# Cross-attention and routed FFN megakernel on one core: answers added one stage earlier, norm 1's moments and the gate in the first batch, one expert product ahead of a wait, the last count one stage later

## The reference, cut to what matters

```python
x = x + xattn(layernorm(x), ctx)        # 16 heads of 64: q = x@Wq, k = ctx@Wk, v = ctx@Wv, softmax, @Wo + bo
x = x + ffn(layernorm(x))               # shared FFN 256->1024->256, plus one of two experts, chosen per token
x = x + attn(layernorm(x), ctx, ctx)    # one head, row mask
x = x + int8_linear(layernorm(x))       # one scale from the largest |value| over all tokens
```

## Time and profile before

| | us |
|---|---|
| runs | 930.33, 926.52, 930.88; median 930.33 |
| the profiled execution's own time | 930.73 |
| its span, first to last instruction | 929.0 |
| TensorE matmul busy | 891.2 (96%) |
| VectorE, ScalarE, GpSimd busy | 595.6, 538.3, 262.0 |
| mean granted TensorE clock | 0.990 |
| chain that ended last | TensorE 90%, VectorE 6%, ScalarE 2%, issue 1%, DMA 1% |

### The profile page before, as it was taken

The page is one execution under the profiler, slowest core; times in us unless marked ns, Lnnn a source line. Parts: engine busy times, 40 slices in busy tenths (PEclk is TensorE's granted clock), DMA queues, the critical chain, the costliest instruction groups (busy, mean ns, idle before and its releaser), DMA issues.

```text
span 929.0 us, 19551 instructions
## 1 busy us (share of the span) xinstructions
PE 891.2 (96%) x6634; PEld 783.2 (84%) x6634; DVE 595.6 (64%) x1603; ACT 538.3 (58%) x1285; POOL 262.0 (28%) x354
## 2 busy tenths in 40 slices
PE   5999999999999999999999999999989999999994
PEld 4788888898888998898889889887878999997763
DVE  6578765666666667666666666665654666437767
ACT  4665556555655656656556555665652455356875
POOL 1343234334433333432434334333000000033200
PEclk9999999999999999999999999999999999999997
DMA  9302000000000000000000000000352043345522
GB/s 277 113 27 109 1 19 22 7 17 5 17 5 21 17 5 17 5 21 17 5 17 5 21 17 5 1 7 6 108 172 85 1 131 126 111 144 163 167 71 80
DMA packets 29500, 50.22 MB, mean 54 GB/s; under 512 B 2960, under 2 KB 24112, under 8 KB 27680
## 3 DMA queue, kind: packets, MB, share of 16 engines
q1 hardware_dynamic: 27920, 45.97, 16.0%
q0 software_dynamic: 1536, 3.67, 1.3%
HBM read 41.37 MB, written 8.26 MB: 53 GB/s over the span
## 4 chain that ended last, share of the span: by engine, by line
PE 90%; DVE 6%; ACT 2%; issue 1%; DMA 1%; another core or an unknown queue 0%; POOL 0%; DVEq 0%
PE bank L1863 27%; PE bank L1892 10%; PE bank L2020 9%; PE bank L2108 9%; PE bank L1911 8%; PE bank L1877 8%; PE bank L1932 5%; PE bank L1836 4%; PE bank L2196 2%; PE bank L2214 2%; PE bank L1845 1%; DVE neg_max L1299 1%; PE bank L1809 1%; PE bank L2072 1%; DVE k_parts L1290 1%
## 5 line engine op out<-in xcount | busy, mean ns | idle before, releaser
L774 POOL TENSOR_TENSOR probs<-probs,row_rcp 112x375 f32<-112x375 f32 x256 | 209.1, 840 | 391.9 <-DVE row_rcp L1305 390.2
L900 ACT ACTIVATE probs<-bank,neg_max 112x375 f32<-112x375 f32 x256 | 144.5, 570 | 56.3 <-DVE neg_max L1299 56.2
L1892 PE MATMUL bank<-ident,probs 112*125 112x112 f32 x768 | 129.2, 278 | 4.0 <-DVE probs_t L1310 4.0
L1892 PEld LDWEIGHTS bank<-ident,probs 112*125 112x125 f32 x768 | 113.3, 187 | 21.3 <-issue 6.2
L1299 DVE TENSOR_REDUCE neg_max<-bank 112x1 f32<-112x375 f32 x256 | 123.3, 540 | 11.1 <-PE bank L1877 10.9
L1310 DVE COPY probs_t<-bank 125x336 f32<-125x336 f32 x128 | 64.8, 507 | 61.1 <-PE bank L1892 57.1
L872 ACT ACTIVATE k_parts<-bank 128x376 fp32r<-128x376 f32 x128 | 62.1, 486 | 66.9 <-PE bank L1863 66.8
L1863 PE MATMUL bank<-ctx_hi,down_hi 128*128 128x376 f32 x256 | 96.7, 378 | 0.5 <-DVE q_parts L1286 0.3
L875 ACT ACTIVATE v<-bank 125x512 f32<-125x512 f32 x96 | 57.5, 599 | 65.1 <-PE bank L1863 65.1
L1290 DVE TENSOR_TENSOR k_parts<-bank,k_parts 128x376 fp32r<-128x376 f32 x128 | 69.9, 547 | 29.6 <-ACT k_parts L872 28.4
L1911 PE MATMUL bank<-probs_t,v 125*64 125x112 f32 x1536 | 87.7, 263 | 0.0
(11 more groups left out here) (237 smaller groups left out, 1984.6 us busy)
## 6 DMA issues: line engine op xcount, KB each, us to landing
ctx_raw<-in_ctx_t SPq DMA_DIRECT2D x16, 375.0 KB, 3.4
stage<-in_ffn_up SPq DMA_DIRECT2D x5, 1024.0 KB, 5.3
stage<-in_ffn_down SPq DMA_DIRECT2D x5, 1024.0 KB, 6.8
ring_late<-in_ctx_t SPq DMA_DIRECT2D x10, 375.0 KB, 6.2
ring_late<-in_ctx_n SPq DMA_DIRECT2D x10, 375.0 KB
routed<-xn SPq DMA_DIRECT2D x1, 2240.0 KB, 9.4
rows_in<-routed SPq DMA_DIRECT2D x5, 448.0 KB, 6.5
answers<-y_rows SPq DMA_DIRECT2D x10, 224.0 KB, 2.8
```

Source lines behind the costliest of these rows:

```text
L774: eng.tensor_tensor(probs[s][:, :], probs[s][:, :], row_rcp[:, s:s + 1].broadcast_to([S, C]), ALU.mult).then_inc(probs_ready, 1)
L900: eng.activation(probs[r][:, :], SCORE_BANKS[i][0:S, 0:C], ACT.Exp, bias=neg_max[:, r:r + 1], accum_out=row_sum[:, r:r + 1]).then_inc(exp_ ...
L1892: t = eng.transpose(turn_bank(i, project)[0:CJ, j * S:(j + 1) * S], probs[QUAD * v + i][:, j * CJ:(j + 1) * CJ], ident[0:S, 0:S])
```

## The change

It has seven edits, in the order of the diff:

- `NORM1_AT`: statistics of step 5 and the aggregations of step 6 move from visit (1, 0, 0) to visit (0, 1, 1), behind step 4.
- ScalarE, s = 1, m = 6: `rows_out(2)` goes ahead of the weight half that is rounded in the same stage.
- VectorE, visit (0, 0, 1): `probs_out(.., 0)` goes ahead of the second pair of row maxima.
- VectorE: the gate's two operations move from visit (1, 0, 0) to visit (0, 1, 1).
- VectorE, `finish_attention`: the places move from n = 4 to n = 5, behind the `idle_*` operations; TensorE's count moves from m = 4 to m = 5.
- VectorE: `y_update` is run at `turn_y_stage(s)` and no longer a stage later (s = 1: m = 4; s = 2: m = 6; s = 8: m = 4), and stands ahead of `piece_lo`, `choose_experts`, `expert_biases` and the norm 3 operations; `rows_rest(2)` goes ahead of `piece_lo`.
- TensorE, visit (15, 1, 1): `up(0, 0)` goes ahead of the wait for ScalarE's copy; `project_out` stays behind it.

```diff
--- before.py
+++ after.py
@@ -557,9 +557,8 @@
         HALF_AT = {1: ("wq", 0), 2: ("wq", 1), 3: ("wo", 0), 4: ("wo", 1), 4 * B - 6: ("up", 0), 4 * B - 5: ("up", 1)}
 
 
-        NORM1_AT = {(0, 0, 1, 0): (0,), (0, 0, 1, 1): (1,), (0, 1, 0, 0): (2,), (0, 1, 1, 0): (3,), (0, 1, 1, 1): (4,),
-                    (1, 0, 0, 0): (5,), (1, 0, 0, 1): (6,), (1, 0, 1, 0): (7,), (1, 0, 1, 1): (8,), (1, 1, 0, 0): (9,),
-                    (1, 1, 1, 0): (10,), (1, 1, 1, 1): (11,)}
+        NORM1_AT = {(0, 0, 1, 0): (0,), (0, 0, 1, 1): (1,), (0, 1, 0, 0): (2,), (0, 1, 1, 0): (3,), (0, 1, 1, 1): (4, 5, 6),
+                    (1, 0, 1, 0): (7,), (1, 0, 1, 1): (8,), (1, 1, 0, 0): (9,), (1, 1, 1, 0): (10,), (1, 1, 1, 1): (11,)}
 
         def half_of(b, c, v, ago):
 
@@ -1053,6 +1052,8 @@
             for s in range(NS):
                 for m in range(MT):
                     relu(s, m)
+                    if m == turn_rows_stage(s) + 1 and s + 1 == FIRST_SLOT:
+                        rows_out(s + 1)
                     if (s, m) in SPLIT_AT:
                         i, h = SPLIT_AT[s, m]
                         if i >= CHOSEN_PIECE:
@@ -1065,7 +1066,7 @@
                         y_out(s - 1)
                     if m == turn_y_stage(s) + 1 and is_slot(s - 1):
                         y_rows_out(s - 1)
-                    if m == turn_rows_stage(s) + 1 and is_slot(s + 1):
+                    if m == turn_rows_stage(s) + 1 and is_slot(s + 1) and s + 1 > FIRST_SLOT:
                         rows_out(s + 1)
                     if s == NS - 1 and m in (5, 6):
                         normalise_group(0, m - 5)
@@ -1353,8 +1354,12 @@
                         rest = rest_for(b, c)
                         if v == 0 and rest is not None:
                             pair_rest(rest, rest % 2 if isinstance(rest, int) else odd)
+
+                        early = first and c == 0 and turning
+                        if early:
+                            probs_out(visit - 1, 0, project)
                         largest_scores(visit, v, 2)
-                        if turning:
+                        if turning and not early:
                             probs_out(visit - 1, 0, project)
                         if c == 1 and v == 0 and not first and not last:
                             norm_stats(norm2, 0, b - 1)
@@ -1394,7 +1399,7 @@
                             else:
                                 eng.wait_ge(scattered, 16 * (b - 1))
                             normalise(1, norm2, b - 1, 0, xn[1])
-                        if c == 0 and v == 0 and second_batch:
+                        if c == 1 and v == 1 and first:
                             eng.wait_ge(small_loaded, 16 * SMALL_LOADS)
                             eng.tensor_tensor(gate_diff[:, :], gate_in[:, :, 1], gate_in[:, :, 0], ALU.subtract) \
                                .then_inc(gate_step, 1)
@@ -1505,7 +1510,7 @@
                     eng.wait_ge(idle_step, 2)
                     eng.tensor_tensor(idle_pair[:, :, :, 1], idle_hid[:, :, :], idle_pair[:, :, :, 0].bitcast(F32),
                                       ALU.subtract).then_inc(idle_step, 1)
-                if n == 4:
+                if n == 5:
                     eng.wait_ge(chosen_ready, B - 1)
                     eng.tensor_tensor(offset[:, :], chosen[:, :], from_end[:, LAST], ALU.mult).then_inc(rank_ready, 1)
                     eng.wait_ge(counted, B - 1)
@@ -1614,6 +1619,10 @@
                                       ALU.subtract).then_inc(hid_ready, 1)
                     if s == 0:
                         finish_attention(m)
+                    if m == turn_y_stage(s) and s >= 1 and not is_slot(s - 1):
+                        y_update(s - 1)
+                    if m == turn_rows_stage(s) + 1 and s + 1 == FIRST_SLOT:
+                        rows_rest(s + 1)
                     if divmod(n - 1, MT) in SPLIT_AT:
                         piece_lo(*SPLIT_AT[divmod(n - 1, MT)])
                     if s == 1 and m == 2:
@@ -1623,9 +1632,7 @@
                         eng.tensor_copy(idle_row[:, :], IDLE_BANK[0:2, 0:2 * D]).then_inc(idle_step, 1)
                     if s == FIRST_SLOT and m == 6:
                         expert_biases()
-                    if m == turn_y_stage(s) + 1 and s >= 1 and not is_slot(s - 1):
-                        y_update(s - 1)
-                    if m == turn_rows_stage(s) + 1 and is_slot(s + 1):
+                    if m == turn_rows_stage(s) + 1 and is_slot(s + 1) and s + 1 > FIRST_SLOT:
                         rows_rest(s + 1)
                     if m == 5 and s in (NS - 3, NS - 2):
                         if s == NS - 2:
@@ -1975,6 +1982,8 @@
                                         eng.wait_ge(xq_split, rest - 1)
                                 unit(later_units, k, 1 - c, bf, odd if c == 0 else 1 - odd)
                         if v == 1 and not (first and c == 0):
+                            if last and c == 1:
+                                up(0, 0)
                             if project:
                                 eng.wait_ge(proj_used[0], later_units.all(0))
                             else:
@@ -1987,8 +1996,6 @@
                                     t = eng.transpose(SUM_BANK[0:S, D + k * P:D + (k + 1) * P], gate_rep[:, k, :],
                                                       ident[:, :])
                                 t.then_inc(gate_turned, 1)
-                            if last and c == 1:
-                                up(0, 0)
                             project_out(u - 1, 1 - c, SUM_BANK)
                         t = tokens_for(b, c)
                         if v == 1 and t is not None:
@@ -2145,6 +2152,7 @@
                         if m == 4:
                             for j in range(2):
                                 turn_tokens(1, B - 2 + j, bank[6][:, KT * S * j:KT * S * (j + 1)], xn[1 - j])
+                        if m == 5:
                             eng.wait_ge(x_added, 2 * B)
                             eng.wait_ge(chosen_ready, B - 1)
                             eng.wait_ge(sum_ready, B - 2)
```

## The result

| | before | after |
|---|---|---|
| runs of the first set | 930.33, 926.52, 930.88, 928.63, 930.77 | 920.87, 919.76, 919.36, 920.40, 919.90 |
| median | 930.33 | 919.90 |
| profiled execution, its span | 930.73, 929.0 | 920.87, 919.0 |
| TensorE matmul busy | 891.2 | 887.3 |
| chain that ended last | TensorE 90%, VectorE 6% | TensorE 90%, VectorE 7% |

The ratio of after to before is 0.9901, 95% interval 0.9883 to 0.9918: faster by 1.0%. (The quotient of the two medians, which differ by 10.4 us, would be 0.9888 and lies within the interval.) The forecast was 921.3, 1.4 above the measured median, with a range that holds it. One of the nine executions of the kernel before in the set of experiments 9 to 11 took 3492.71 us; the ratios leave it out.

The account below looks back on a forecast made before the run. TensorE was taken to bound the kernel; six idle times and one clock stretch (1.70) against +0.15 in segment 8 sum to -9.1 us: 921.7 from the profiled 930.73, 921.3 from the median 930.33, range 917.7 to 925.3.

Parts of the forecast that it names:

- The bound: Whole kernel: TensorE is busy 891.2 of 929.0 us, so only its 38 us idle and lower-clock stretches can be won.
- The six idle times: TensorE's waits at places the diff touches, all to go: 0.72 + 1.47 + 0.84 + 0.72 + 3.15 + 0.61 = 7.5 us.
- The cover: Moved or delayed VectorE work fits idle room: visit (0,1,1) keeps 1.35 us, segment 1's weight half fits 1.55, late maxima cost nothing.
- The clock behind segment 1: The 3.4 us lower-clock stretch from 689.3, behind the 3.15 us idle time, goes with it: -1.70 us.
- The clock at 641.5: The 3.4 us lower-clock stretch behind the 0.84 us wait at up(0,0) stays, so no gain was counted.
- rival 1: The clock fall at 641.5 goes too, as up(0,0) fills the idle time directly ahead: 919.6 us, chance 0.22.
- Segment 8: The update now delays the root operations by 1.28 us; one TensorE wait goes, another grows: net +0.15, bounds -1.0 and +1.3.
- Rival 3: Slower: places end 4.2 us later, so scatters and slot rows may come too late; 933 us at a 20 us scatter, chance 0.03.
- Rival 4: No change that can be told: idle times go, but what lies behind has no slack; 926 to 930 us, chance 0.09.
- Rival 2: Clock falls behind segment 1 all the same, or another wait replaces the removed one: 923 to 926 us, chance 0.20.

Follow-up runs that it names:

- experiment 9: Changed kernel with two ring loads of segment 8 moved behind the merge of group 1: 922.75 us, ratio 0.9949.
- experiment 10: Changed kernel with segment 7's update behind the 13 root operations and the early copy also in visits (0,1,1) and (1,1,1): 917.59 us, ratio 0.9893.
- experiment 11: Kernel of experiment 10 with the two ring loads of experiment 9 moved as well: 920.08 us, ratio 0.9925.
- experiment 1: Changed kernel with the update of segment 0 back at stage 5, behind the weight half: 926.05 us, ratio 0.9959.
- experiment 3: Changed kernel with up(0,0) behind the wait again: 921.55 us, ratio 0.9918.
- experiment 5: Changed kernel with the moved statistics, aggregations and the gate's two operations back in the second batch: 922.23 us, ratio 0.9915.
- experiment 6: Changed kernel with the copy of visit (0,0,1) behind all four maxima again: 923.16 us, one execution.
- experiment 7: Changed kernel with TensorE's count and VectorE's places back in stage 4 of segment 0: 922.50 us, one execution.
- experiment 8: Changed kernel with ScalarE's copy and VectorE's rest of the slot rows behind the weight half again: 925.23 us, one execution.
- experiment 2: Kernel before with only the update of segment 0 moved to stage 4: 924.86 us, ratio 0.9949.
- experiment 12: Changed kernel once more, unedited, in another set of runs: 917.79 us, ratio 0.9889 to the kernel before.
- Experiment 4: Changed kernel with the update of segment 7 behind the 13 root operations instead of ahead: 919.48 us, ratio 0.9896.

## Why the prediction was right, point by point

*The bound.* Right. TensorE's idle times and its clock were all that could be won; the other engines' busy times stayed.

*The six idle times.* All six went. Experiments 1, 3, 5, 6, 7 and 8 each undid one step and got back 3.15, 0.84, 1.47, 0.72, 0.72 and 0.60 us, the sizes of the earlier trace rows to 0.01. Each term was short: 1.3 us in all by the ledger, of which the overlap is 1.0. The sum should have taken an idle time with the 0.17 us that a matmul without a wait starts earlier.

*The cover.* Right. Visit (0,1,1) kept 1.23 us of room (1.35 forecast), segment 1's weight half stayed ahead of the next rest, and the two maxima behind the copy cost nothing that TensorE saw.

*The clock behind segment 1.* Right for the two traces: taken away with the wait (-1.53; -1.70 forecast), and brought back with it. That it would cost 1.70 if it came again was too little there; the fall of experiment 1 lasted twice as long and cost 2.9. And by the mean clocks a term of -1.70 is for an execution that has the fall, which some don't.

*The clock at 641.5.* This is the step that failed, though the time came out within the range: "by the rows, I let the first go and the second stay". The first here is the fall behind 3.15 us of idle time, the second that behind 0.84. The second went too, as in rival 1, worth 1.38 us, and the measured 919.9 lies 0.3 from rival 1's 919.6. But rival 1's reason, the filled idle time, didn't hold either: with that idle time left in, experiments 2 and 3 show no fall. One profiled execution with a fall is weak evidence that the kernel has one. The Trainium skill, in "TensorE: Matmul & The Clock Gate", Part 1 (how oscillation bites in real kernels), lays the lower clock to long gaps. The two traces with a gap of 3.15 us agree; falls behind gaps of 1.35 us in segment 8 come in some traces and not in others, and that behind 0.84 came once in three.

*Segment 8.* Sign and mechanism right, the size not: +0.32 in place of +0.15 in the first trace. The term assumed that ScalarE would wait 0.1 to 0.2 us for the roots; it waited 2.34, and 1.10 in experiment 12, where its own delays are absent and TensorE waits 0.23 us. The room that the term counted on came from such a delay: in the trace of before TensorE's product of stage 5 ended at 842.41 and ScalarE took it up at 844.66, just ahead of the normalisation at 845.71 in the earlier trace rows. So more than half of the 2.34 us goes with the delays, by the two traces, and 1.10 with the update ahead of the roots. Experiment 4 shows the remedy.

*The tail.* The sum had no term for it. Its stretch at the lower clock took 13.6 us in place of 10.2 and gave back 1.2 us. In experiment 12 the same code had 10.2 us: it varies from one execution to the next.

*The rivals.* Rival 3, late rows, is ruled out: SyncE's first row load followed the weight load by 0.38 us, not the 3 us that I had named as the sign, so the scatters had landed within 3.2 us of the last issue's end. I had taken 5.0 from the gather. (A slip there: 673.8 and 6.5 are 680.3, not 681, so the mechanism would have begun to cost at 9 us and not at 8. No chance hangs on it.) Rival 4 fell with the ratio. Rival 2's fall behind segment 1 is seen only when the update is put back.

So the total came out close in part by luck, because errors offset each other: 1.4 (clock at 641.5) and 1.3 (six places) too little gain, against 1.2 (tail), 0.3 (opening), 0.2 (segment 8) and 0.2 (clock behind segment 1) too little loss. That leaves the profiled execution 0.8 below the 921.7 forecast for it. In the set of experiment 12 the same kernel had 917.79, at the very edge of the range; the ratio to its own set's kernel before, 0.9889, is the steadier figure.

## What to carry to other kernels

Find each idle time of the bounding engine and the one instruction it waits for; moving that instruction ahead of its neighbours on its in-order queue is worth the idle time and a little more, as the six experiments that each undo one step show here, provided that what it overtakes has room. Don't apply such a move to every call of a helper: the same "update a stage sooner" that won 3.15 us in segment 1 hurt in segment 8, where a chain of small dependent operations stood behind it. Don't count a fall of the clock as certain from one trace: even behind 3.15 us of waiting some executions have none, and the mean clock of every execution tells how many. And compare kernels that differ by under 0.5% within one set of runs.

## What the runs showed of the hardware that was not expected

**ScalarE starts late in segment 8 in some executions.** In 10 of the 14 profiled executions ScalarE's first instruction of stage 2 or 3 starts 1.0 to 3.1 us after TensorE's product has ended, with a free engine and its input ready; in four it starts 0.04 us after it. The kernel after, where the product of stage 3 ended at 825.30, and then the same code in experiment 12, where it ended at 824.77:

```profile
824.40 0.63 ACT L1048 ACTIVATE hid_hi<-bank,b_col 128x448 fp32r<-128x448 f32 x1
826.76 0.63 ACT L1046 ACTIVATE hid<-bank,b_col 128x448 f32<-128x448 f32 x1 [1.74 <-PE bank L2027]
```

```profile
824.81 0.64 ACT L1046 ACTIVATE hid<-bank,b_col 128x448 f32<-128x448 f32 x1 [1.27 <-PE bank L2027]
```

The four are experiments 9 to 12, of the last two sets of runs, with the ring loads moved (two) and unmoved (two). A small transfer of the queue that the page calls "instruction" lies near that point in all 14, with and without delay. So neither the ring loads nor that transfer is shown to be the cause; that the delay comes by set and not by kernel is all that the runs say, and as each of the last four sets had a chip of its own, they can't tell the chip from the set. With the update ahead of the roots, TensorE's wait for the second pair of rows is 1.27 to 1.36 us in the seven traces with the delay, and 0.23 and 0.32 in the two without. In experiments 1, 6 and 8 a fall of the clock follows besides; in experiment 7, with gaps of the same kind, none does.

**The lower clock comes in lengths.** In the body it lasted 3.4 us five times and 6.8 once, and where it begins during the wait for the largest value 10.2 or 13.7. Two executions of the same code differed by such a length in the tail. For the kernel before it goes with the scatter: of its 19 executions in the set of experiments 1 to 4, the four with a mean clock of 0.994 took 926.28 to 929.15 us, the four with 0.990 or less 930.32 to 933.09. For the changed kernel it doesn't explain the two sets: at 0.994 it took 919.36 to 920.40 us in one and 917.67 to 918.73 in the other.
